# Decoder layer on one core: the near-Gram fold goes to GpSimd and ScalarE, the retrieval streams one block, two loads go behind the last row writes

## The chip, the cores and the metric

One Trainium2 chip, one core of it. The metric is the device time of one execution in microseconds (us); lower is better. Three runs of the kernel before gave a median of 910.58 us (910.43 to 911.65).

## The reference, cut to what matters

Input x is 8 x 512 x 256 in float32, with a context of the same shape and an integer mask of 8 x 512 x 512. Three blocks follow one another, each with a residual.

```
# block 1: layernorm twice, projection to q, k, v, beta (16 heads of 16), keys normalised
def step(S, (q_t, k_t, v_t, beta_t)):          # 512 steps, S: 16 x 16 per head and batch
    retrieval = S k_t
    S = S + outer(beta_t * (v_t - retrieval), k_t)
    return S, S q_t
x = x + (normed x + scan_out @ w_out + b_out)
# block 2: attention of layernorm(x) over the context, masked, then layernorm * gamma + beta
# block 3: int8-quantised activations (scale from a 99.5% quantile), ternary weights, gelu
```

## The kernel before, in words

**The scan.** The 512 steps are cut into 32 chunks (NCK) of 16 steps (CT). Inside a chunk the delta rule is a unit lower triangular system per head, batch and feature: the sixteen update vectors of the chunk depend on each other through the Gram matrix of the keys, scaled by beta. `solve(j)` on VectorE works it out by blocks: at t = 8 a block of 8 x 8 (the far Gram, straight from PSUM), at t = 4 and 12 blocks of 4 x 4, at t = 2, 6, 10 and 14 two steps at once against four earlier ones, at odd t single steps. Every step waits for the one before it.

For t = 2, 6, 10, 14 the coefficients lie in G3, which is prepared for the next chunk between two solves: `scale_near` multiplies the near Gram matrix in PSUM by beta (lines 1345 and 1347), `scale_pairs` writes the pair coefficients G4 (1353) and copies every second one, scaled, into G3 (1355), and `fold_near` adds the product of G3's first row and G4 to G3's second row (1363 and 1365). All that is VectorE's. In the same stretch VectorE normalises keys (1326), turns them (1395) and the updates (1331), and makes the key products for the next Gram matrices (`far_products` 1378, `near_products` 1388 and 1391, whose outputs TensorE sums by head). Its last act before the next solve is `start_chunk(m)` (1402), which waits for `ret_mm`.

**What start_chunk waits for.** TensorE does, in this order after a solve: `state` (the outer products into the state, 1902, waits for the turned updates), `turn` (2046), `values` (1998), `updates_turned` (1912) and `retrieval` (1941), whose last matmul raises `ret_mm`. The retrieval is 64 matmuls in float32 (two records each, 128 in the trace), four for each head, one on each diagonal 32 x 32 tile. The moving operand of a head is taken from `padded`, in which blocks of zeros lie between the blocks of keys and queries: it streams the zeros ahead of its own block, its own 32 columns and the zeros behind them (96 columns; 64 for the first and last head), so the neighbours' columns in PSUM get zeros added. Behind the retrieval, beside VectorE's solve, TensorE does `key_sums` (2007), attention within the chunk (1967) with the far Gram matmuls (1925) between its two parts, outputs (2024), projections (1976), the near Gram (1919, 1920), `norms_turned` (1951) and the output projection (2038).

**The other engines.** ScalarE, in chunk j: `updates_out` (710), `key_copied_out` (748), `state` (copies of the state by parity, 701, for which the retrieval waits), `updates_turned` (718), `queries_by_parity` (789), `scaled_by_feature` (780), `key_sums_out` (743), early work of later stages, then `attention_out` (726). GpSimd: `mask_attention` (537) as soon as the solve is done (`u_done`), the residual's bias (596), `x_added` (557), which releases the chunk's rows by `x_done`, and `key_norms` (547, 548, 550), which waits for ScalarE's line 743. These queues are in order; the order is written out by hand in each engine's block.

**SyncE's queue.** For each chunk it waits for `x_done` and writes eight blocks of rows to `xs` (471). At the last chunk it first waits for `u_done` and issues `context(2)`: the context and mask of the third batch, 0.5 and 1 MB (453, 454); after the last eight writes and `o_mm` it issues `context(3)`.

**After the scan.** 32 tiles of attention follow in a fixed order of steps (n). At step 2 VectorE runs `last_stats` (1419), which waits until all writes to the last quarter of `xs` have landed. `least(n)` (1443) is VectorE's part of the softmax, `logits` (2096) and `attend` (2117) TensorE's. The third batch's context is first read at steps 4 and 5 (`context_piece`, 2065).

Of the kernel before, what the change touches and what calls it, by code (L numbers as in the profile page):

```python
# [14 lines left out]
P = 128  # L15
# [120 lines left out]
def decoder(nc, x, ctx, mask, ln_g, ln_b, w_qkvb, b_qkvb, w_out, b_out, x_gamma, x_beta,  # L136
# [8 lines left out]
    with ExitStack() as stack:  # L145
# [75 lines left out]
        zeros = kexp_flat[:, 0:NH * 2 * HD]  # L221
        wq_s = wq_flat.rearrange("p (c n) -> p c n", c=DC)
# [161 lines left out]

        found, edge_marked, marks_summed = sem("found"), sem("edge_marked"), sem("marks_summed")
# [51 lines left out]
        def _(sp):  # L437
# [18 lines left out]
            for j in range(NCK):  # L456
                w, c = j // 8, j % 8
                if j == 21:
                    sp.wait_ge(tern_ready, 8)
                    for b in range(2):  # L460
                        context(b)
                if j == NCK - 2:
                    sp.wait_ge(ret_mm, NCK)
                    for t, vec in ((xg_s, x_gamma), (xb_s, x_beta), (fg_s, f_g), (fb_s, f_b)):
                        sp.dma_start(t[:, :], everywhere(vec)).then_inc(const_in, 16)
                if j == NCK - 1:
                    sp.wait_ge(u_done, NCK)
                    context(2)
                sp.wait_ge(x_done, j + 1)
                for b in range(B):  # L470
                    sp.dma_start(xs[c * CT:(c + 1) * CT, w * B + b, :], xc[b * CT:(b + 1) * CT, j, :]).then_inc(xs_in[w], 16)
            sp.wait_ge(o_mm, NCK)
# [14 lines left out]
        def _(pool):  # L487
# [99 lines left out]

            own(G.memset(half, -0.5))
# [3 lines left out]
            for j in range(NCK):  # L592
                pool.wait_ge(u_done, j + 1)
                mask_attention(j)
                pool.wait_ge(xr_ready, j + 1)
                G.tensor_tensor(xc[:, j, :], xc[:, j, :], bb_s, ALU.add).then_inc(xb_ready, 1)
                if j >= 1:
                    x_added(j - 1)
                if j + 3 < NCK:
                    key_norms(j + 3)  # L600
                if j in FACTORS_AT:
                    late_inputs(FACTORS_AT[j])
                if j in ROW_NORMS_AT:
                    row_norms(ROW_NORMS_AT[j])
                if 12 <= j < 16:
                    for p in range(2 * (j - 12), 2 * (j - 12) + 2):
                        bounded_weights(p)
# [84 lines left out]
        def _(act):  # L692
# [29 lines left out]
            def attention_out(j, f):  # L722
# [3 lines left out]
                A.activation(attn[j % 2][:, f * 512:(f + 1) * 512], ps[(2, 0)[f]][:, :], ACT.Copy).then_inc(att_out, 1)  # L726

# [300 lines left out]
            for j in range(NCK + 1):  # L1028
# [5 lines left out]
                if j >= 1 and exists(j):  # L1034
                    state(j)
                if exists(j - 1):
                    updates_turned(j - 1)
# [135 lines left out]
        def _(v):  # L1173
# [100 lines left out]
            def solve(j, between):  # L1274
# [6 lines left out]
                for t in range(1, CT):  # L1281
# [7 lines left out]
                    elif t % 4 == 2:  # L1289
                        a = t // 4  # L1290
                        part = prod[:, 0:NH * 8].rearrange("p (h t s) -> p h t s", t=2, s=4)
# [58 lines left out]
            def scale_pairs(m):  # L1350

                bt = beta[m % 4]
                own.issue(V.tensor_tensor(G4, psG[:, 768:896], bt.rearrange("p (q t) -> p q t", t=2)[:, :, 1], ALU.mult))
# [167 lines left out]
            for j in range(NCK + 1):  # L1521
# [24 lines left out]
                if exists(j + 1):  # L1546
                    fold_near(j + 1)
# [324 lines left out]
        def _(pe):  # L1872
# [55 lines left out]
            def retrieval(m):  # L1928
# [6 lines left out]
                for h in range(NH):  # L1935
                    if h % (NH // 2) == 0:
                        pe.wait_ge(state_copied, 2 * m - 1 + h // (NH // 2))
                    a, b = 1 if h == 0 else 0, 2 if h == NH - 1 else 3
                    for r in range(4):
                        rows = slice(32 * r, 32 * r + 32)  # L1940
                        last = M.matmul(into[rows, h - 1 + a:h - 1 + b], scopy[rows, h, :], streams[rows, h, a:b],  # L1941
# [216 lines left out]
            for j in range(NCK + 1):  # L2158
# [17 lines left out]
                if j == NCK:  # L2176
# [4 lines left out]
                    pe.wait_ge(ctxT_ready, 4)  # L2181
                if exists(j):
                    attention(j, 0)
                    far_gram(j, 0)
                    far_gram(j, 1)
                    attention(j, 1)
# [178 lines left out]
```

## Time and profile before

| What | us |
|---|---|
| median of 3 runs | 910.58 |
| profiled execution, whole | 912.2 |
| its span in the trace | 910.1 |
| busy in the span: TensorE, VectorE, ScalarE, GpSimd | 786.4, 763.6, 567.7, 439.8 |
| mean granted clock of TensorE, share of full | 0.952 |

The profile is of one execution, which took 912.2 us; 2.1 us of that lie outside the span. The scan runs from about 28 to 558 us of the span, the attention from there to about 720, the quantised block after it. The groups of instructions give a mean duration for each line; a line is that of the kernel's source. An engine's timeline shows in brackets how long it sat idle before a piece and what ended that. In the chain of waits each piece is what the end of the program really hung on at that moment.

### The profile page before, as it was taken

The numbers are of one execution on the slowest core, as the hardware profiler recorded it, in microseconds if no ns is written. First come the engines' busy times: TensorE is split into PE (matmuls) and PEld (weight loads), VectorE is DVE, ScalarE is ACT, GpSimd is POOL, SyncE is SP. The second block draws the span as 40 slices with busy tenths as digits, with TensorE's granted clock in tenths as the row PEclk, the third lists the DMA queues.
The fourth block names the chain that finished last, engine by engine and source line by source line (L and its number), as shares of the span: only waits on it lengthen the run. The fifth ranks groups of instructions, "written<-read, shape, count | busy, mean of one in ns | idle before, by whom it ended". The sixth has DMA issues, their size and how long they took to land.

```text
span 910.1 us, 31226 instructions
## 1 busy us (share of the span) xinstructions
PE 786.4 (86%) x12291; PEld 583.0 (64%) x12291; DVE 763.6 (84%) x2383; ACT 567.7 (62%) x1505; POOL 439.8 (48%) x472
## 2 busy tenths in 40 slices
PE   7799999999999999999999998799999506994385
PEld 7477777777777777777777776466666304442364
DVE  3789999999988999899899986566777786999897
ACT  4576777765766666667566644357777533993294
POOL 5346546643454545434435433548788733950000
PEclk9899999999999999999999999999999956997599
DMA  9800000000000000022000001432200000000023
GB/s 185 158 2 15 9 11 13 8 14 10 10 14 8 12 12 8 13 86 73 14 9 12 12 8 37 145 133 76 71 1 1 1 0 1 1 1 1 0 80 106
DMA packets 28616, 31.24 MB, mean 34 GB/s; under 512 B 5548, under 2 KB 23864, under 8 KB 28472
## 3 DMA queue, kind: packets, MB, share of 16 engines
q1 hardware_dynamic: 28256, 29.12, 12.1%
q8 instruction: 98, 1.61, 0.8%
q14 instruction: 46, 0.38, 0.1%
q10 hardware_dynamic: 216, 0.14, 0.1%
HBM read 20.85 MB, written 4.19 MB: 28 GB/s over the span
## 4 chain that ended last, share of the span: by engine, by line
DVE 48%; PE 42%; issue 6%; ACT 2%; POOL 1%; DVEq 0%; ACTq 0%; POOLq 0%
DVE arena L1306 7%; DVE arena L1314 7%; PE psY L1941 5%; PE ps L2096 4%; PE psX L1941 4%; DVE arena L1292 4%; DVE arena L1295 4%; PE ps L1902 3%; PE psX L2117 3%; DVE arena L1288 3%; DVE arena L1287 3%; DVE arena L1317 3%; PE psY L2117 2%; PE ps L2302 2%; PE psG L2096 2%
## 5 line engine op out<-in xcount | busy, mean ns | idle before, releaser
L537 POOL TENSOR_TENSOR arena<-arena 128x1024 f32<-128x1024 f32 x32 | 75.8, 2370 | 178.3 <-DVE arena L1295 178.3
L548 POOL TENSOR_TENSOR work<-work,half 128x16 f32<-128x16 f32 x32 | 97.9, 3061 | 2.7
L1314 DVE TENSOR_REDUCE arena<-arena 128x64 f32<-128x256 f32 (+1 forms) x96 | 65.9, 687 | 3.3
L1925 PE MATMUL psG<-arena 128*128 128x512 f32 x128 | 64.7, 629 | 0.0
L726 ACT ACTIVATE arena<-ps 128x512 f32<-128x512 f32 x64 | 34.7, 594 | 46.6 <-PE ps L1967 46.4
L547 POOL TENSOR_SCALAR work<-work 128x16 f32<-128x16 f32 x32 | 8.1, 252 | 103.7 <-ACT work L743 103.7
L1976 PE MATMUL ps<-arena 128*128 128x128 f32 x384 | 49.8, 279 | 2.9 <-ACT arena L726 1.5
L1976 PE MATMUL ps<-nT,arena 128*128 128x128 f32 x384 | 49.4, 279 | 3.3 <-ACT nT L780 1.2
L1976 PEld LDWEIGHTS ps<-arena 128*128 128x128 f32 x384 | 45.7, 192 | 6.3 <-ACT arena L726 5.5
L2096 PE MATMUL ps<-arena,nT 128*128 128x512 f32 x84 | 42.7, 632 | 7.6 <-issue 5.2
L1976 PEld LDWEIGHTS ps<-nT,arena 128*128 128x128 f32 x384 | 45.2, 192 | 5.9 <-ACT arena L726 4.4
L772 ACT ACTIVATE arena<-ps,columns 128x128 f32<-128x128 f32 x64 | 20.1, 364 | 45.6 <-PE ps L1976 45.6
L1902 PEld LDWEIGHTS ps<-work 32*32 32x32 f32 x1984 | 29.9, 105 | 26.6 <-issue 26.6
L1902 PE MATMUL ps<-work 32*32 32x64 f32 x1984 | 34.0, 215 | 14.7 <-DVE work L1331 14.7
L1967 PEld LDWEIGHTS ps<-work 32*64 32x64 f32 x1024 | 27.9, 132 | 28.3 <-issue 27.5
L1131 ACT ACTIVATE arena<-ps,small 128x512 f32<-128x512 f32 x64 | 41.8, 690 | 6.5 <-PE ps L2302 5.7
L1967 PE MATMUL ps<-work 32*64 32x128 f32 x1024 | 43.5, 282 | 2.1 <-ACT arena L780 1.8
L1941 PE MATMUL psY<-work,arena 32*32 32x96 f32 (+1 forms) x2048 | 44.4, 238 | 1.0 <-issue 0.6
L962 ACT ACTIVATE arena<-arena 128x512 f32<-128x512 f32 x32 | 23.1, 721 | 33.7 <-DVE arena L1443 33.6
L1941 PEld LDWEIGHTS psY<-work,arena 32*32 32x32 f32 x2048 | 41.5, 105 | 4.1 <-issue 4.1
L1306 DVE TENSOR_TENSOR arena<-psG,arena 128x1024 f32<-128x1024 f32 x32 | 39.2, 1224 | 4.3 <-PE psG L1925 3.2
L1941 PE MATMUL psX<-work,arena 32*32 32x96 f32 (+1 forms) x1920 | 41.6, 239 | 0.0
(358 smaller groups left out, 2410.2 us busy)
## 6 DMA issues: line engine op xcount, KB each, us to landing
arena<-in_mask_BxSxS_ik SPq DMA_DIRECT2D x8, 1024.0 KB, 6.7
xs<-arena SPq DMA_DIRECT2D x256, 16.0 KB, 1.9
arena<-in_ctx SPq DMA_DIRECT2D x8, 512.0 KB, 4.2
out<-xs SPq DMA_DIRECT2D x32, 128.0 KB, 1.7
arena<-in_x SPq DMA_DIRECT2D x8, 288.0 KB, 13.4
arena<-in_L_ffn_w SPq DMA_DIRECT2D x2, 1024.0 KB, 19.0
arena<-in_x SPq DMA_DIRECT2D x16, 96.0 KB, 5.2
arena<-in_L_attn_w_qkvb SPq DMA_DIRECT2D x2, 512.0 KB, 5.3
```

Source lines behind the costliest of these rows:

```text
L537: G.tensor_tensor(keys, keys, same_half.rearrange("p (a t) -> p a t", a=1).broadcast_to([P, NH, HALF]), ALU.mult).then_inc(att_masked, 1)
L548: own(G.tensor_tensor(root, length, half, ALU.pow))
L1131: A.activation(gT[:, n * 512:(n + 1) * 512], ps[n % 3][:, :], ACT.Gelu, scale=deq[:, 0:1]).then_inc(gabs, 1)
L1306: mult = V.tensor_tensor(part, src, C16[:, :, t - n:t].rearrange("p h (a s) -> p h a s", a=1).broadcast_to([P, NH, n, n]), ALU.mult)
L1314: own(V.tensor_reduce(sums, part, AX.X, ALU.add))
L1902: last = M.matmul(psS[rows, b * 64:b * 64 + 64], kt[rows, b * 32:b * 32 + 32], utm[rows, b * 64:b * 64 + 64], start=False, stop=True, skip ...
L1925: M.matmul(psG[:, f * 512:(f + 1) * 512], block16[:, :], PF[m % 2][:, f * 512:(f + 1) * 512], start=True, stop=True).then_inc(g1_mm, 1)
L1941: last = M.matmul(into[rows, h - 1 + a:h - 1 + b], scopy[rows, h, :], streams[rows, h, a:b], start=False, stop=True, skip_group_check=True)
L1967: last = M.matmul(ps[(2, 0)[r % 2]][tokens, first:first + P].rearrange("p (e t) -> p e t", e=2), kq[j % 4][rows, f * P + HALF * u:f * P + ...
L1976: last = M.matmul(out[:, f * P:(f + 1) * P], wq_s[:, c, first:first + P], nT[m % 4][:, c, :], start=c == 0, stop=c == DC - 1)
L2096: last = M.matmul(logit_bank(n), nT[n % 2][:, c, :], ctxT[b % 2][:, c, :], start=c == 0, stop=c == DC - 1)
L2117: last = M.matmul(psO[n % 2], probT[n % 2][:, u * P:(u + 1) * P], ctx_s[b % 4][:, u, :], start=u == 0, stop=u == NW - 1)
```

## The change

- `fold_near` for chunks from 1 on is taken from VectorE's block and put into GpSimd's, behind `mask_attention`; it writes a new scratch tile and GpSimd waits for `pre2` ahead of it and for its own first half ahead of the second. Chunk 0 keeps the old way.
- `scale_pairs` for chunks from 1 on issues one operation, G4; the copy of its odd entries into G3 becomes an activation on ScalarE, `pairs_copied_over`, behind the state copies.
- `solve(j)` waits at t = 2 for both.
- The retrieval streams one block, 32 columns, per matmul instead of up to three.
- In chunk 0 the two far Gram matmuls go ahead of the first half of the attention; in the other chunks the order is as it was.
- SyncE issues `context(2)` behind the last eight row writes, then `context(3)` with no wait on `o_mm`.

```diff
+        folded = kexp_flat[:, NH * 2 * HD:NH * 2 * HD + P]
...
-                if j == NCK - 1:
-                    sp.wait_ge(u_done, NCK)
-                    context(2)
                 sp.wait_ge(x_done, j + 1)
                 for b in range(B):
                     sp.dma_start(xs[...], xc[...]).then_inc(xs_in[w], 16)
-            sp.wait_ge(o_mm, NCK)
+            context(2)
             context(3)
...
+            def fold_near(m):                                    # GpSimd
+                pool.wait_ge(pre2, m + 1)
+                pairs = folded.rearrange("p (q s) -> p q s", s=2)
+                G.tensor_tensor(pairs, g3[:, :, 0, 0:2],
+                                G4.rearrange("p (q a b) -> p q a b", a=2, b=1)[:, :, 1].broadcast_to([P, NH * 4, 2]),
+                                ALU.mult).then_inc(folds, 1)
+                pool.wait_ge(folds, m)
+                G.tensor_tensor(g3[:, :, 1, 0:2], g3[:, :, 1, 0:2], pairs, ALU.add).then_inc(near_folded, 1)
...
                 mask_attention(j)
+                if j + 1 < NCK:
+                    fold_near(j + 1)
                 pool.wait_ge(xr_ready, j + 1)
...
+            def pairs_copied_over(m):                            # ScalarE
+                act.wait_ge(pre2, m + 1)
+                A.activation(G3.rearrange("p (q t s) -> p q t s", t=2, s=4)[:, :, 1, 2],
+                             G4.rearrange("p (q a) -> p q a", a=2)[:, :, 1], ACT.Copy).then_inc(pairs_copied, 1)
...
                     state(j)
+                    pairs_copied_over(j)
...
                     elif t % 4 == 2:                             # VectorE, solve
                         a = t // 4
+                        if t == 2 and j >= 1:
+                            v.wait_ge(near_folded, j)
+                            v.wait_ge(pairs_copied, j)
...
             def scale_pairs(m):                                  # VectorE
+                if m >= 1:
+                    V.tensor_tensor(G4, psG[:, 768:896], bt..., ALU.mult).then_inc(pre2, 1)
+                    return
...
-                if exists(j + 1):
-                    fold_near(j + 1)
...
-                    a, b = 1 if h == 0 else 0, 2 if h == NH - 1 else 3      # TensorE, retrieval
                     for r in range(4):
-                        last = M.matmul(into[rows, h - 1 + a:h - 1 + b], scopy[rows, h, :], streams[rows, h, a:b],
+                        last = M.matmul(into[rows, h], scopy[rows, h, :], streams[rows, h, 1],
...
+                if j == 0:
+                    far_gram(j, 0)
+                    far_gram(j, 1)
                 if exists(j):
                     attention(j, 0)
+                if exists(j) and j >= 1:
                     far_gram(j, 0)
                     far_gram(j, 1)
```

## Rows read from the trace of the kernel before

**Rows 1.** The page: busy us, share and instructions of each engine.
```profile
PE 786.4 (86%) x12291; PEld 583.0 (64%) x12291; DVE 763.6 (84%) x2383; ACT 567.7 (62%) x1505; POOL 439.8 (48%) x472
```

**Rows 2.** Chain of waits, end of one chunk's gap: start us, us, what.
```profile
331.38 2.71 PE psX L1941 x128
...
334.11 0.62 DVE arena L1402 x2
```

**Rows 3.** VectorE's timeline before the same start_chunk: start, us, engine, line, idle before.
```profile
330.49 0.25 DVE L1353 TENSOR_TENSOR arena<-psG,arena 128x128 f32<-128x128 f32 x1
330.67 0.26 DVE L1355 TENSOR_TENSOR arena<-psG,arena 128x64 f32<-128x64 f32 x1
330.84 1.21 DVE L1378 TENSOR_TENSOR arena<-ps,work 128x1024 f32<-128x1024 f32 x1
...
333.10 0.28 DVE L1363 TENSOR_TENSOR arena<-arena 128x128 f32<-128x128 f32 x1
333.41 0.29 DVE L1365 TENSOR_TENSOR arena<-arena 128x128 f32<-128x128 f32 x1
334.11 0.61 DVE L1402 SCALAR_TENSOR_TENSOR arena<-psX,columns,arena 128x128 f32<-128x128 f32 x2 [0.41 <-PE psX L1941]
```

**Rows 4.** Line 1402, whole span: idle before it by releaser, us and times.
```profile
  PE psY L1941: 9.3, 15
  PE psX L1941: 6.0, 14
```

**Rows 5.** VectorE, line 1402 of the last chunk.
```profile
547.21 0.61 DVE L1402 SCALAR_TENSOR_TENSOR arena<-psY,columns,arena 128x128 f32<-128x128 f32 x2 [2.44 <-PE psY L1941]
```

**Rows 6.** TensorE's timeline where that chunk's state update begins.
```profile
328.80 1.10 PE L1902 MATMUL ps<-work 32*32 32x64 f32 x64 [0.48 <-DVE work L1331]
```

**Rows 7.** TensorE by line and form, 200 to 400 us.
```profile
L1941 PE MATMUL psX<-work,arena 32*32 32x96 f32 x720 | 16.3, 241 | 0.0
L1902 PE MATMUL ps<-work 32*32 32x64 f32 x768 | 13.1, 215 | 5.8 <-DVE work L1331 5.8
```

**Rows 8.** GpSimd's and ScalarE's timelines, same chunk.
```profile
328.26 2.36 POOL L537 TENSOR_TENSOR arena<-arena 128x1024 f32<-128x1024 f32 x1 [5.93 <-DVE arena L1295]
...
334.89 0.25 POOL L547 TENSOR_SCALAR work<-work 128x16 f32<-128x16 f32 x1 [2.90 <-ACT work L743]
...
329.96 1.14 ACT L701 ACTIVATE arena<-ps,nparity 128x128 f32<-128x128 f32 x4 [0.24 <-PE ps L1902]
...
334.62 0.18 ACT L743 ACTIVATE work<-ps 128x16 f32<-128x16 f32 x1 [1.27 <-PE ps L2007]
```

**Rows 9.** Two windows: us, PE, PEld, DVE, ACT, POOL busy, clock, DMA share, GB/s.
```profile
240.00:360.00 120.00, 114.72 (x2430) 88.75 (x2419) 108.75 (x305) 78.57 (x237) 58.98 (x53) 1.00 0.05 11
...
584.00:586.00 2.00, 2.00 (x3) 0.97 (x4) 0.91 (x3) 0.82 (x2) 1.83 (x5) 0.50 0.02 4
```

**Rows 10.** Chunk 0: timelines of TensorE and VectorE.
```profile
33.05 0.67 PE L1967 MATMUL ps<-work 32*64 32x128 f32 x16 [1.85 <-ACT arena L780]
33.65 3.25 PE L1925 MATMUL psG<-arena 128*128 128x512 f32 x4
...
37.00 1.23 DVE L1306 TENSOR_TENSOR arena<-psG,arena 128x1024 f32<-128x1024 f32 x1 [3.25 <-PE psG L1925]
```

**Rows 11.** After the scan: SyncE's queue, then VectorE and TensorE.
```profile
568.70 0.51 SPq L454 DMA_DIRECT2D arena<-in_mask_BxSxS_ik  x1
569.25 4.96 SPq L471 DMA_DIRECT2D xs<-arena  x8
...
578.64 2.71 DVE L1419 BATCH_NORM_STATS2 stats<-xs 128x6 f32<-128x256 f32 x8 [4.06 <-DMA xs<-arena]
...
583.83 3.62 PE L2096 MATMUL ps<-arena,nT 128*128 128x512 f32 x4 [5.23 <-issue]
...
589.91 1.96 PE L2096 MATMUL ps<-arena,nT 128*128 128x512 f32 x4
```

**Rows 12.** The page: median time from issue to landing of the row writes.
```profile
xs<-arena SPq DMA_DIRECT2D x256, 16.0 KB, 1.9
```

More of the change, by code:

```diff
@@ L383, in decoder @@
              "h_ready h_last habs_ready cand_taken").split()]
+        folds, near_folded, pairs_copied = sem("folds"), sem("near_folded"), sem("pairs_copied")
         found, edge_marked, marks_summed = sem("found"), sem("edge_marked"), sem("marks_summed")
@@ L1352, in scale_pairs @@
                 bt = beta[m % 4]
+                if m >= 1:
+                    V.tensor_tensor(G4, psG[:, 768:896], bt.rearrange("p (q t) -> p q t", t=2)[:, :, 1],
+                                    ALU.mult).then_inc(pre2, 1)
+                    return
                 own.issue(V.tensor_tensor(G4, psG[:, 768:896], bt.rearrange("p (q t) -> p q t", t=2)[:, :, 1], ALU.mult))
@@ L2181, in _ @@
                     pe.wait_ge(ctxT_ready, 4)
+                if j == 0:
+                    far_gram(j, 0)
+                    far_gram(j, 1)
                 if exists(j):
                     attention(j, 0)
+                if exists(j) and j >= 1:
                     far_gram(j, 0)
                     far_gram(j, 1)
+                if exists(j):
                     attention(j, 1)
```

## The prediction

> **What bounds the kernel now.** I read the page first: TensorE and VectorE are both busy for over four fifths of the span [rows 1], so neither share says which one binds. The chain of waits does. In every chunk of the scan it runs through VectorE's solve, then TensorE's state update, values and retrieval, and back to `start_chunk` at line 1402. One chunk's gap between two solves ends with the retrieval, 2.71 us, and then line 1402 at 334.11 [rows 2]. VectorE's own timeline shows what it did meanwhile: its last preparation (1365) ended at 333.70, and it sat idle 0.41 us until TensorE's retrieval let it go [rows 3]. So two branches start at the end of a solve and meet at line 1402: TensorE's is the longer by 0.41 us, VectorE's is right behind. Over the whole span the idle time before line 1402 is 9.3 + 6.0 = 15.3 us in 29 waits [rows 4], 2.44 us of it in the last chunk [rows 5]. Chunk starts lie 16.41 us apart almost throughout. The reading that matters: a cut on VectorE alone gives nothing, a cut in the retrieval alone gives 0.4 us a chunk, both together give the smaller of the two new branches.
>
> **VectorE's branch.** Line 1355 goes: its successor starts 330.84 - 330.67 = 0.17 us behind it [rows 3]. Lines 1363 and 1365 go: from 333.10 to 333.70, 0.60 us. Together 0.77 us; with the idle 0.41 us, line 1402 can come 1.18 us earlier, if TensorE allows it. The two new waits at t = 2 cost nothing if they are met; the solve has such a wait at t = 8 already and its operation follows as closely as the others.
>
> **TensorE's branch.** 64 matmuls, 128 records, stream 32 columns in place of 96 (64 at the ends). No row has 32 columns on these tiles, so I work from two. `state` (1902) streams 64 columns in the same kind of tile, 64 records in 1.10 us [rows 6], each lasting 215 ns [rows 7]: (1100 - 215) / 63 = 14.0 ns from start to start, or 56 ns for each of the four tiles in turn. The retrieval: (2710 - 241) / 127 = 19.4 ns, 78 ns a tile. So 32 columns more cost 22 ns a tile, and 32 fewer should give 34 ns a tile, 8.6 ns a record: 127 x 8.6 + 200 = 1.29 us, a saving of 1.42 us. The bounds: nothing is saved if a record costs what it does now (2.71 us); if no record can follow another in less than the 14.0 ns of `state`, the retrieval takes 127 x 14.0 + 200 = 1.98 us and saves 0.73. I take 1.42, because both known forms lie on the line that streaming gives and neither shows a floor. The Trainium skill (TensorE: Matmul & The Clock Gate, "What overlaps and what doesn't" and the mechanism above it) puts the offset between matmuls on different tiles at about 4 ns, which would allow this; no row here has it.
>
> The smaller branch decides: VectorE's 1.18 us against TensorE's 1.42. VectorE becomes the bound, with TensorE 0.24 us behind. TensorE waits 0.48 us for the solve's result already [rows 6], so its work beside the solve has room.
>
> **GpSimd's and ScalarE's new work** I cost at nothing, and name the cover. GpSimd ends `mask_attention` at 330.62 [rows 8]; G4 is known at 330.49 + 0.25 = 330.74 [rows 3]. Two operations of 128 elements: between 0.25 us (16 elements, line 547) and 2.36 us (1024, line 537) each; by size 0.48 us [rows 8]. So the fold ends near 331.8; t = 2 of the next solve came at about 334.8 and will come at 333.6. Room: 1.8 us; with both operations at 1.3 us it is still met. Behind the fold wait the bias, `x_added` and through it SyncE's writes, which slip by 1.1 us, and `key_norms`, which sat idle 2.90 us for ScalarE anyway. ScalarE's copy of 64 elements lies between the 0.18 us of line 743 and the 0.29 us (1.14 / 4) of line 701 [rows 8]; I take 0.2. It stands behind the state copies (331.10), after G4 is known, so it adds no wait; what queues behind it is line 718, 789 and 780, and ScalarE then sat idle 1.27 us before line 743. That idle shrinks by 1.4 (earlier retrieval) and 0.2, to about nothing: this is what is late next, on a path (key norms) that has 3 us to spare on GpSimd.
>
> **The scan's sum.** Thirty periods end with `start_chunk(2)` to `(31)`. For 29 of them: 29 x 0.77 = 22.3 us, plus the idle that goes, 15.3 - 2.4 = 12.9, less about 1 us of the few waits well over 0.41 that TensorE's hiccups make and will make again: 34.2. The last chunk has no key work on VectorE, TensorE's branch binds there [rows 5], and it gains the 1.4 us of the retrieval. Scan: 35.6 us. TensorE's granted clock was 1.00 in the scan, the 2.4 GHz level, with TensorE busy 114.7 of 120 us [rows 9]; I take it as kept.
>
> **Chunk 0.** VectorE waited 3.25 us at t = 8 for the far Gram matmuls, which ran from 33.65 behind an attention part that had itself waited 1.85 us for ScalarE [rows 10]. Moved ahead they can run in that wait: the block starts at about 33.8 and not 37.0. The near Gram matmuls hang on VectorE's products behind that block, and the next keys on those, so all moves by 3.2 us; the 0.77 us comes on top, since VectorE bound that start too; and the far Gram (3.25 us here, against some 2 in later chunks) shows the 1.2 GHz level, part of which a shorter idle may give back: 0 to 1.3, I take 0.6. Chunk 0: 4.6 us (bounds 3.2 to 5.4).
>
> **After the scan.** SyncE issued `context(2)` just ahead of the last eight writes, and `last_stats` waited 4.06 us for those to land, at 578.64 [rows 11]. With the order turned round the writes are issued 1.2 us earlier and nothing large lies ahead of them: last issue near 573.0, landing 1.9 us later [rows 12], 574.9, against 574.6 when VectorE asks. Gain 3.7 us. TensorE idled 5.23 us there, and the next four matmuls took 3.62 us in place of 1.96 [rows 11], with a granted clock of 0.50, the 1.2 GHz level [rows 9]. With 1.5 us of idle that should not fall: 1.6 us. The moved loads: context and mask of two batches issue behind the writes, about 5 us later than `context(2)` did; they are read from step 4, near 590, and land by 584 or so. Cover gone, it would cost the difference. Sum 5.3 us (bounds 0 to 5.7).
>
> **Total.** 35.6 + 4.6 + 5.3 = 45.5. The profiled execution took 912.2, so 866.7; that execution is 1.6 above the median, so against the median 865.1. I say 866.
>
> **Rivals.**
> - *A floor under the small matmuls.* If a record costs 14.0 ns however few its columns, TensorE's branch saves only 0.73 us: 29 x 0.73 + 0.7 + 4.6 + 5.3 = 32, which gives 879; floors between put it between. For it: no denser row exists. Against: `state` sits just where its 64 columns put it, so 14.0 need not be a floor. The Trainium skill (TensorE: Matmul & The Clock Gate, "Wait — 56ns, not 53.3ns?") says start-to-start never drops below about 25 ns however small N is. If that held across tiles, 128 records would take 3.2 us, more than now; the 14.0 ns of `state` speak against it.
> - *The retrieval gains nothing* (nothing saved per record, or the edit is not what limits it). Then only chunk 0 and the end gain: 912.2 - 9.9 = 902.
> - *The clock falls: slower.* The streamed zeros keep TensorE occupied. If less activity let the clock go to 1.2 GHz through state, values and retrieval, 1.10 + 1.48 + 1.29 = 3.87 us would double: per chunk 3.87 - 1.42 = 2.45 us worse than now, 30 x 2.45 - 10 = +64, so 976. It decides once the clock costs over 1.5 us a chunk. Against: TensorE stays busy nearly throughout, and the clock was seen low only after idle of several us [rows 9, 11].
> - *The new wait at t = 2 replaces the old one.* If GpSimd's pair took 3.8 us in place of 1.0, it would cost about 1 us a chunk: 895.
>
> **How the numbers follow.** Forecast case (VectorE binds, 860 to 870): 0.52. Floor (870 to 884): 0.30. No gain from the retrieval or a late fold (885 to 905): 0.10. Slower by the clock: 0.05. No measurable change: 0.02. The rest is better than 860. The range 860 to 884 holds the first two. A measurement of this kernel tells 0.2%, 1.8 us, from nothing: faster 0.93, same 0.02, slower 0.05.
>
> **What would show it.** Chunk starts 15.2 us apart; the idle before line 1402 gone but in the last chunk; the retrieval near 1.3 us with 8 to 9 ns a record; no idle at line 1292 for GpSimd; the far Gram of chunk 0 ahead of 33; `last_stats` idle under 0.5 us and the matmuls behind it at 1.96. I am wrong if the idle before line 1402 stays (floor), if line 1292 shows a wait, or if the granted clock in the scan leaves 1.00.

## The result, and the profile after

The changed kernel takes 902.9 us (median of 4: 901.5, 902.4 and 903.3 at a mean granted clock of 0.927, and 927.9 at 0.900) against 910.5: a ratio of 0.9909 [0.9884, 0.9933], 8.3 us less. The forecast was 866.0, with a range of 860 to 884. Medians here and below take in every execution of a kernel; ratios and their intervals leave out those that lie over 1.5% above the fastest one of their kernel. The profiled execution took 901.47 us, with a span of 899.6. The page:

```profile
PE 766.0 (85%) x12284; PEld 548.1 (61%) x12291; DVE 743.7 (83%) x2290; ACT 572.5 (64%) x1536; POOL 465.2 (52%) x534
PE 47%; DVE 40%; issue 7%; ACT 4%; POOL 1%; DVEq 0%; ACTq 0%; POOLq 0%
PEclk9889998998999999999999999999999757997599
```

VectorE has 20 us less to do and GpSimd 25 more, as the fold would have it [rows 1]. TensorE's busy time is the odd one: the retrieval is busy 43.9 us where it was 85.9, 42 less, and TensorE as a whole only 20 less. In the line of the granted clock the scan, slices 2 to 24, has four slices under 0.9; before it had one. Two windows of the scan say where (us, then PE, PEld, DVE, ACT, POOL busy, granted clock, DMA share, GB/s):

```profile
120.00:240.00 120.00, 112.26 (x2397) 79.05 (x2396) 100.85 (x274) 78.37 (x254) 63.51 (x69) 0.90 0.05 10
240.00:360.00 120.00, 112.68 (x2581) 84.33 (x2582) 110.86 (x301) 85.88 (x263) 70.59 (x70) 1.00 0.05 12
```

The second answers to [rows 9]: clock 1.00, as before. In the first it is 0.90, and VectorE is busy a tenth less in the same time. So there are chunks of two kinds. One where the clock holds, TensorE's and VectorE's timelines:

```profile
253.93 0.59 DVE L1427 SCALAR_TENSOR_TENSOR arena<-psY,columns,arena 128x128 f32<-128x128 f32 x2
257.94 1.22 DVE L1327 TENSOR_TENSOR arena<-psG,arena 128x1024 f32<-128x1024 f32 x1
...
254.07 0.61 PE L2029 MATMUL ps<-arena 128*128 128x8 f32 x4 [0.21 <-DVE arena L1416]
254.61 0.67 PE L1989 MATMUL ps<-work 32*64 32x128 f32 x16
255.20 1.98 PE L1948 MATMUL psG<-arena 128*128 128x512 f32 x4
```

Line 1427 is `start_chunk` (1402 before). It follows with no idle time in front of it, and so does the operation at t = 8 (1327), which needs the far Gram matmuls (1948, before 1925). And one where it falls, first TensorE, then VectorE (the operation at t = 8, and `keys_normed` behind the solve), then TensorE's clock microsecond by microsecond:

```profile
166.93 1.29 PE L1963 MATMUL psX<-work,arena 32*32 32x32 f32 x128
169.10 0.61 PE L2029 MATMUL ps<-arena 128*128 128x8 f32 x4 [0.89 <-DVE arena L1416]
169.64 0.68 PE L1989 MATMUL ps<-work 32*64 32x128 f32 x16
170.25 3.63 PE L1948 MATMUL psG<-arena 128*128 128x512 f32 x4
...
173.99 1.23 DVE L1327 TENSOR_TENSOR arena<-psG,arena 128x1024 f32<-128x1024 f32 x1 [1.05 <-PE psG L1948]
181.93 0.42 DVE L1347 TENSOR_TENSOR work<-work,ps 128x256 f32<-128x256 f32 x1 [0.66 <-ACT arena L752]
```

```profile
169.00:170.00 1.00, 0.90 (x16) 0.88 (x20) 0.93 (x5) 0.25 (x2) 0.23 (x1) 1.00 0.00 0
170.00:171.00 1.00, 1.00 (x13) 0.43 (x9) 0.90 (x3) 0.97 (x3) 0.90 (x2) 0.72 0.07 16
171.00:172.00 1.00, 1.00 (x3) 0.36 (x2) 0.90 (x4) 0.97 (x4) 1.00 (x1) 0.50 0.19 47
172.00:173.00 1.00, 1.00 (x3) 0.30 (x1) 0.84 (x4) 0.77 (x3) 1.00 (x1) 0.50 0.09 18
```

The retrieval takes the forecast 1.29 us. Behind it TensorE is idle for 0.89 us, waiting for VectorE's key products (1416), runs key sums and attention at full speed, and then the granted clock drops to 0.50, the 1.2 GHz level. The four far Gram matmuls take 3.63 us in place of 1.98. VectorE waits 1.05 us for them at t = 8, and 0.66 us more at `keys_normed`, since TensorE's work behind them, and with it ScalarE's keys (752), is late too. That is 1.71 of the 1.8 us by which such a chunk is longer: chunk starts lie 15.22 us apart where the clock holds and nothing else comes in, and 17.0 where it falls. Only six of the nineteen periods without a slow group are that short (15.21 to 15.26); the middle one of the nineteen is 15.53.

Of the 31 far Gram groups behind a retrieval 11 are slow, 16.7 us in all; before the change none is. There is a second loss. In the scan from 60 us on, 12 gaps on TensorE of over 0.45 us (11.7 us in all) wait for no other engine; before there is one, of 0.64 us. One of them, in TensorE's timeline:

```profile
217.96 1.19 PE L1963 MATMUL psY<-work,arena 32*32 32x32 f32 x117
220.78 0.31 PE L1963 MATMUL psY<-work,arena 32*32 32x32 f32 x11 [1.64 <-issue]
```

What these gaps wait for can be read from the traces all the same. The page counts the packets that carry instructions, here for the changed kernel and for `half_32` below, whose TensorE has 3472 records less:

```profile
q8 instruction: 98, 1.61, 0.8%
```

```profile
q8 instruction: 85, 1.39, 0.7%
```

That is 16 KB a packet, one for every 250 or so of TensorE's 24575 matmul and weight-load records, and 13 packets less for 3472 records less: queue 8 carries TensorE's instructions. Count all that the trace has of TensorE, its waits included, in the order of the starts. All 79 gaps of over 0.45 us in the scans of fourteen profiles, those of the two kernels and of every run below, end at the same place in a block of 256: at number 193, 194 or 195, counted from 0. Each of them also ends 1.2 to 1.6 us behind the end of a packet on that queue, a stretch that takes up 7% of the changed kernel's scan. The one above ends 1.42 us behind a packet that took 0.94 us. So TensorE stands at the edge of a block and waits for the next one. From 60 us on the scan has 81 such edges, and 30 of them lie inside a retrieval, which with its weight loads is 256 records long and now takes 1.29 us instead of 2.74.

After the scan, SyncE's queue, `last_stats` on VectorE (1444, before 1419 in [rows 11]) and the logits behind it:

```profile
554.72 10.44 SPq L470 DMA_DIRECT2D xs<-arena  x16
565.21 0.58 SPq L455 DMA_DIRECT2D arena<-in_ctx  x1
567.40 2.71 DVE L1444 BATCH_NORM_STATS2 stats<-xs 128x6 f32<-128x256 f32 x8
572.59 1.96 PE L2118 MATMUL ps<-arena,nT 128*128 128x512 f32 x4 [1.21 <-issue]
```

The writes are issued ahead of the context, `last_stats` no longer waits, and the matmuls behind it take 1.96 us, not 3.62, behind an idle time of 1.21 us, not 5.23.

**Where the time went**, from one profile to the other, by chunk starts: the lead-in 0.1 us less; chunk 0, 25.22 to 22.78, 2.4 less; the thirty periods behind it, 493.79 to 489.17, 4.6 less; from the end of the last solve to the second set of logits behind `last_stats` 5.7 less. That is 12.9 us, of which 10.5 is left at the end of the span: behind those logits the first 110 us are the same in both (TensorE busy 106.81 us), and in the 80 us behind them, in the quantised block, the granted clock is 0.70 in place of 0.74. Most of the miss is in the thirty periods: 4.6 us in place of 35.6, which is 31.0 of the 34.8 us by which the profiled execution missed the forecast.

### The profile page after: what moved, and what is told of

Read it like the earlier page. It is cut to its first block, busy times and chain, and to the rows that moved or that the text cites. A ratio compares the mean times of both kernels' runs of the same rounds, so it can differ in the third digit from the quotient of the medians.

```text
span 899.6 us, 31219 instructions
## 1 busy us (share of the span) xinstructions
PE 766.0 (85%) x12284; PEld 548.1 (61%) x12291; DVE 743.7 (83%) x2290; ACT 572.5 (64%) x1536; POOL 465.2 (52%) x534
## 4 chain that ended last, share of the span: by engine, by line
PE 47%; DVE 40%; issue 7%; ACT 4%; POOL 1%; DVEq 0%; ACTq 0%; POOLq 0%
PE ps L1998 5%; PE psG L1948 5%; PE ps L2118 4%; DVE arena L1327 4%; DVE arena L1335 4%; PE psX L2139 3%; PE psY L2139 3%; PE ps L2329 2%; PE ps L1989 2%; DVE arena L1403 2%; DVE arena L1313 2%; DVE arena L1316 2%; PE psG L2118 2%; DVE arena L1413 2%; PE psG L1942 2%
## 5 line engine op out<-in xcount | busy, mean ns | idle before, releaser
L547 POOL TENSOR_TENSOR work<-work,half 128x16 f32<-128x16 f32 x32 | 95.9, 2998 | 2.7
L1948 PE MATMUL psG<-arena 128*128 128x512 f32 x128 | 80.0, 758 | 0.0
L1327 DVE TENSOR_TENSOR arena<-psG,arena 128x1024 f32<-128x1024 f32 x32 | 39.2, 1224 | 15.2 <-PE psG L1948 14.4
L1989 PE MATMUL ps<-work 32*64 32x128 f32 x1024 | 46.0, 292 | 4.1 <-issue 3.9
L1948 PEld LDWEIGHTS psG<-arena 128*128 128x128 f32 x128 | 25.6, 220 | 26.6 <-issue 26.6
L1313 DVE TENSOR_TENSOR arena<-arena 128x128 f32<-128x128 f32 x128 | 37.9, 296 | 4.4
L1316 DVE TENSOR_REDUCE arena<-arena 128x32 f32<-128x128 f32 x128 | 36.6, 286 | 4.4
L2329 PE MATMUL ps<-work 128*128 128x512 bf16 x124 | 37.9, 385 | 2.2 <-ACT work L1144 2.1
```

The lines of the kernel that those rows point to most:

```text
L547: own(G.tensor_tensor(root, length, half, ALU.pow))
L1313: own(V.tensor_tensor(part, g3h[:, :, a].rearrange("p h (t s) -> p h t s", s=4), C16[:, :, 4 * a:4 * a + 4].rearrange("p h (a s) -> p h a ...
L1316: last = V.tensor_reduce(C16[:, :, t:t + 2], part, AX.X, ALU.add)
L1327: mult = V.tensor_tensor(part, src, C16[:, :, t - n:t].rearrange("p h (a s) -> p h a s", a=1).broadcast_to([P, NH, n, n]), ALU.mult)
L1948: M.matmul(psG[:, f * 512:(f + 1) * 512], block16[:, :], PF[m % 2][:, f * 512:(f + 1) * 512], start=True, stop=True).then_inc(g1_mm, 1)
L1989: last = M.matmul(ps[(2, 0)[r % 2]][tokens, first:first + P].rearrange("p (e t) -> p e t", e=2), kq[j % 4][rows, f * P + HALF * u:f * P + ...
```

## The experiments

Each run is compared with runs of the kernel before on the same chip (medians 910.7, 911.2 and 910.7 us in the three batches). The table is read from the profiled executions: typical distance of two chunk starts; slow far Gram groups (over 2.4 us) of the 31 behind a retrieval; gaps of TensorE inside a retrieval of over 0.45 us that wait for no other engine. Each count is of one execution. Two runs, the halved retrievals, are single executions.

| kernel | us, median | ratio | start to start, us | slow groups (extra us) | gaps |
|---|---|---|---|---|---|
| before | 910.5 | | 16.41 | 0 | 1 |
| changed | 902.9 | 0.9909 [0.9884, 0.9933] | 15.22 / 17.0 | 11 (16.7) | 8 |
| before_32 | 924.4 | 1.0055 [1.0011, 1.0098] | 15.9 / 17.2 | 15 (23.2) | 6 |
| after_96 | 902.6 | 0.9912 [0.9888, 0.9936] | 16.41 | 1 (1.2) | 1 |
| after_64 | 888.1 | 0.9765 [0.9707, 0.9822] | 15.66 | 1 (1.2) | 5 |
| after_48 | 888.6 | 0.9734 [0.9677, 0.9792] | 15.3 to 15.9 in most | 4 (5.2) | 4 |
| after_fill2 | 896.3 | 0.9816 [0.9755, 0.9876] | 15.5 to 18 | 6 (8.6) | 12 |
| after_fill4 | 907.8 | 0.9948 [0.9909, 0.9988] | 16.0 | 1 (1.8) | 11 |
| half_96 | 869.2 | (one execution) | 15.35 | 1 (1.2) | 0 |
| half_32 | 919.3 | (one execution) | 17.05 | 27 (40.1) | 3 |
| sp_only | 907.4 | 0.9958 [0.9931, 0.9984] | 16.40 | 0 | 0 |
| far_only | 906.7 | 0.9957 [0.9932, 0.9983] | 16.41 | 0 | 0 |
| after_again | 911.4 | 0.9899 [0.9836, 0.9962] | 15.36 / 17.0 | 15 (23.0) | 6 |
| after_64_again | 891.0 | 0.9796 [0.9729, 0.9863] | 15.66 | 0 | 3 |

The two theories at the start: (A) the short retrieval leaves TensorE too little to do and its clock falls; (B) the fold, or the waits it added, is what makes some chunks long.

### One half of the change at a time: before_32 and after_96

`before_32` is the kernel before with the short retrieval alone, `after_96` the changed kernel with the old, wide one. The edit of the first; the second is its reverse:

```diff
-                    a, b = 1 if h == 0 else 0, 2 if h == NH - 1 else 3
                     for r in range(4):
                         rows = slice(32 * r, 32 * r + 32)
-                        last = M.matmul(into[rows, h - 1 + a:h - 1 + b], scopy[rows, h, :], streams[rows, h, a:b],
+                        last = M.matmul(into[rows, h], scopy[rows, h, :], streams[rows, h, 1],
                                         start=False, stop=True, skip_group_check=True)
```

> The kernel before with one edit: the retrieval streams only its own 32 columns. Theory (too little work passes through TensorE around the retrieval, so the granted clock falls behind it): the clock in the scan leaves 1.00 in part of the chunks, the far Gram matmuls of those take 3.6 us in place of 1.98, and the gain of 0.4 us a chunk that VectorE leaves (12 us in all) is eaten or more: 905 to 925 us. Rival (the clock falls only with the fold gone from VectorE, or with the new waits on GpSimd and ScalarE): the clock stays at 1.00, chunk starts 16.0 us apart, about 898 us.

> The changed kernel with the old retrieval of up to 96 columns, everything else kept. Theory (columns of the retrieval hold the clock): granted clock 1.00 through the scan, chunk starts 16.4 us apart, VectorE idle some 1.2 us before start_chunk, and about 902 us from chunk 0 and the end alone: no slower than the changed kernel. Rival (the moved fold, its waits or the shortened VectorE work disturb the clock): clock under 1.00 in the scan here too and over 910 us.

The short retrieval by itself makes the old kernel slower, by 0.6% [0.1, 1.0] in the ratio and by 1.5% in the median. Its ten executions take 910.8 to 949.6 us, with a mean granted clock of 0.885 to 0.933; the 24 of the kernel before beside it all have 0.947 to 0.954. Its slow and fast chunks are like those of the changed kernel, one of the slow ones on TensorE's timeline:

```profile
103.31 1.29 PE L1940 MATMUL psX<-work,arena 32*32 32x32 f32 x128
...
106.81 3.68 PE L1925 MATMUL psG<-arena 128*128 128x512 f32 x4
```

There is no fold on GpSimd in this kernel and no wait for it, so (B) falls. And the fold without the short retrieval leaves chunk starts at 16.41 us: VectorE's 0.77 us turn into idle time in front of `start_chunk`, as its waits show (us, times):

```profile
  PE psY L1964: 24.3, 16
  PE psX L1964: 15.9, 15
```

That is 40.2 us against 15.3 before [rows 4], or 24.9 more in 31 waits, 0.80 each (one gap of TensorE of 3.1 us is in it). All of this kernel's 8 us come from the two other parts of the change.

### A retrieval between the two: after_64, after_48

`after_64` streams 64 columns of every head, one block of zeros beside the head's own. `after_48` does that for odd heads and 32 for even ones.

```diff
+                    a, b = (1, 3) if h < NH - 1 else (0, 2)    # after_64
+                    a, b = (1, 2) if h % 2 == 0 else (0, 2)    # after_48
...
-                        last = M.matmul(into[rows, h], scopy[rows, h, :], streams[rows, h, 1],
+                        last = M.matmul(into[rows, h - 1 + a:h - 1 + b], scopy[rows, h, :], streams[rows, h, a:b],
```

> The changed kernel, but each matmul of the retrieval streams 64 columns, its own block and one block of zeros. By the line through 64 and 96 columns it takes 1.98 us, chunk starts 15.7 us apart, VectorE idle 0.4 us before start_chunk. Theory: with TensorE busy without a gap the clock holds, and 30 x 0.73 us come on top of what 96 columns give: about 880 us, below both kernels. Rival (the clock needs all 96 columns, or idle is not what matters): the clock falls in part of the chunks and it lands between 890 and 905 us.

> The changed kernel with 32 columns for even heads and 64 for odd ones: the retrieval takes some 1.6 us. Theory: chunk starts 15.3 us apart where the clock holds; whether it holds lies between the changed kernel (often not) and the form of 64 columns (nearly always): 875 to 890 us. Rival (any retrieval under 64 columns loses the clock as often as the changed kernel): 900 us and more.

Both beat both kernels, though `after_64` stays 8 us above the 880 expected: its thirty periods are 16.0 us long on average, not 15.7, mostly for gaps in five of its retrievals and three behind them. With 64 columns TensorE is the bound again, and the clock stays. From `after_64`, the timelines (retrieval and far Gram matmuls, then `start_chunk` between them), and a window of the scan with the columns as above:

```profile
251.45 1.99 PE L1964 MATMUL psX<-work,arena 32*32 32x64 f32 x128
254.50 1.98 PE L1948 MATMUL psG<-arena 128*128 128x512 f32 x4
...
253.50 0.61 DVE L1427 SCALAR_TENSOR_TENSOR arena<-psX,columns,arena 128x128 f32<-128x128 f32 x2 [0.36 <-PE psX L1964]
```

```profile
240.00:360.00 120.00, 114.63 (x2510) 86.74 (x2508) 108.70 (x296) 83.52 (x257) 68.18 (x70) 1.00 0.05 12
```

128 records in 1.99 us, (1990 - 215) / 127 = 14.0 ns each: the price of `state`. Chunk starts lie 15.66 us apart, 0.75 less than before, where the floor rival had said 0.73. The columns that are now streamed for nothing cost 0.44 us a chunk against the 15.22 of a chunk that keeps its clock, and spare the 1.8 us of one that doesn't. The one slow group comes behind a gap; the four of `after_48` are more than that and fewer than 11, in one execution each.

### More work behind the short retrieval: after_fill2, after_fill4

The changed kernel with two or four matmuls of 128 columns and zero weights behind each retrieval; they add nothing to the result.

```diff
                     retrieval(j)
+                    for _ in range(2):    # 4 in after_fill4
+                        M.matmul(psR[(j - 1) % 2][:, 0:P], zeros[:, 0:P], ones[:, :], start=False, stop=True,
+                                 skip_group_check=True)
```

> The changed kernel (32 columns) with 2 extra matmuls of 128 columns (zero weights, added to a bank nobody reads then) right behind the retrieval, where TensorE sat idle 0.5 to 0.9 us: 4 records, about 0.45 us. Theory (the clock falls because TensorE does too little between the state update and the far Gram): the falls get fewer, chunk starts 15.2 us apart where it holds; 870 to 890 us. Rival (what counts is the retrieval itself): as the changed kernel, 903 us.

> The same with 4 extra matmuls, about 0.9 us, as long as TensorE's idle time. Theory: the clock stays at 1.00 throughout, chunk starts 15.2 us apart, 30 x 1.18 us on top of chunk 0 and the end: about 866 us, what I had forecast for the change. Rival: as the changed kernel, 903 us, or worse by what the extra work delays (0.2 us a chunk, 6 us).

The number of slow groups goes from 11 to 6 and to 1 with the work added, which again speaks for (A). The times don't follow: 896.3 us lies above the 870 to 890 expected, and 907.8 us is what the rival had said, not 866. The work stands in TensorE's queue ahead of key sums and attention, ScalarE's keys come late (with four, `keys_normed` waits 12.7 us in 22 chunks), the gaps stay, and what the clock gives back goes there. The ten executions of `after_fill4` are spread over 897 to 913 us, with a mean granted clock of 0.949 down to 0.928. The profiled one is the fastest, with the 0.949, so the single slow group says little of the others, and that four matmuls hold the clock is shown for that execution alone.

### Clock or gaps: half_96, half_32

Slow groups and gaps came together so far. These two part them. Both are the changed kernel with the retrieval of nine heads only (72 matmuls; that of the other seven is left out), one with 96 columns and one with 32:

```diff
+                    if h % 2 and h < NH - 1:
+                        continue
+                    a, b = 1 if h == 0 else 0, 2 if h == NH - 1 else 3    # half_96
+                    a, b = 1, 2                                           # half_32
```

> The changed kernel with a retrieval for nine of the sixteen heads only (the even ones and the last; the retrieval of the other seven is left out), each streaming up to 96 columns: 72 records instead of 128, about 1.5 us. Two things are told apart, by the trace of the scan alone: the gaps over 0.45 us inside or behind the retrieval in which TensorE waited for nothing shown (12 in the changed kernel, 1 in the one before), and the clock. Theory (the gaps come where instructions are used up faster than they arrive): with 72 in place of 128 records at 20 ns each the gaps all but vanish, 0 to 3. The clock then holds in nearly all chunks, starts 15.2 to 15.4 us apart. Rival (the gaps belong to the shorter cycle or to something else that the change added): some ten gaps again.

> The same nine heads with 32 columns each: 72 records in about 0.75 us; the other seven heads' retrieval is left out. Theory of the clock: it falls at least as often as in the changed kernel (11 of 31 chunks with far Gram matmuls over 2.4 us), now with few gaps, so that the fall needs no gap: 10 or more slow chunks. Rival (the clock falls only behind such a gap): as the gaps vanish, so do the slow chunks.

The same instructions on every engine, and 50 us between them: 869.2 and 919.3. TensorE's timeline of one chunk, first with 96 columns (the row names the 64 of its first head), then with 32:

```profile
308.75 1.58 PE L1966 MATMUL psX<-work,arena 32*32 32x64 f32 x72
310.61 0.61 PE L2032 MATMUL ps<-arena 128*128 128x8 f32 x4 [0.28 <-DVE arena L1416]
311.15 0.67 PE L1992 MATMUL ps<-work 32*64 32x128 f32 x16
311.75 1.99 PE L1948 MATMUL psG<-arena 128*128 128x512 f32 x4
```

```profile
304.98 0.82 PE L1966 MATMUL psX<-work,arena 32*32 32x32 f32 x72
307.15 0.61 PE L2032 MATMUL ps<-arena 128*128 128x8 f32 x4 [1.35 <-DVE arena L1416]
307.69 0.67 PE L1992 MATMUL ps<-work 32*64 32x128 f32 x16
308.29 3.68 PE L1948 MATMUL psG<-arena 128*128 128x512 f32 x4
```

and VectorE at t = 8 of the second, 312.08:

```profile
312.08 1.22 DVE L1327 TENSOR_TENSOR arena<-psG,arena 128x1024 f32<-128x1024 f32 x1 [1.09 <-PE psG L1948]
```

In both VectorE sets the pace: in front of `start_chunk` it waits for TensorE once, in the last chunk. The retrieval's shorter time only makes TensorE idle for longer, 1.35 us in place of 0.28, and right behind that the clock falls, in 27 of 31 chunks. Over 240 to 360 us (columns as above, `half_96` first):

```profile
240.00:360.00 120.00, 115.41 (x2214) 86.82 (x2214) 112.52 (x309) 86.83 (x269) 70.41 (x72) 1.00 0.05 11
```

```profile
240.00:360.00 120.00, 110.20 (x2001) 77.31 (x2001) 99.10 (x268) 76.82 (x235) 60.34 (x65) 0.88 0.04 10
```

So the clock alone, with hardly a gap (three in 31 retrievals), takes a chunk from 15.35 to 17.05 us. The thirty periods last 511.6 us in place of 463.3, 48.3 of the 50.1 us. The loss stays 1.7 us even where less of the slow stretch falls on the far Gram group: in chunk 28 that takes 3.13 us, VectorE waits only 0.54 us for it, and then 1.11 us at `keys_normed`. The other way round, `half_96` has no gap and one slow group, in chunk 1, and lands at 869.2 us where the sum of the prediction had come to 866: with the clock kept, the rest of that sum holds. What the pair can't tell apart is the streaming that is gone and the idle time that takes its place; the one always turns into the other here. In 31 retrievals of 72 records there are no such gaps with 96 columns and three with 32; in 31 of 128 records with 32 columns six and eight. The block edges fit: with 72 records 15 of them lie inside a retrieval, with 128 it is 30. A gap comes where a long row of tiny matmuls uses up its instructions faster than the next block arrives. No run changed how they arrive.

### The two parts outside the scan: sp_only, far_only

`sp_only` is the kernel before with the context and mask of the third and fourth batch moved behind the last writes, `far_only` the kernel before with chunk 0's far Gram matmuls ahead of its attention.

```diff
-                if j == NCK - 1:
-                    sp.wait_ge(u_done, NCK)
-                    context(2)
...
-            sp.wait_ge(o_mm, NCK)
+            context(2)
             context(3)
```

```diff
+                if j == 0:
+                    far_gram(j, 0)
+                    far_gram(j, 1)
                 if exists(j):
                     attention(j, 0)
+                if exists(j) and j >= 1:
                     far_gram(j, 0)
                     far_gram(j, 1)
```

> The kernel before with one edit: the third batch's context and mask are issued behind the last eight row writes. Theory: last_stats no longer waits 4.06 us, the matmuls behind it run at 1.96 us and not 3.62: 5.7 us less, 904.9 us. Rival (the DMA queues were the bound, or the loads now come too late): under 2 us of change.

> The kernel before with one edit: in chunk 0 the far Gram matmuls go ahead of the first half of the attention. Theory: VectorE's wait of 3.25 us at t = 8 of chunk 0 goes, but part comes back ahead of keys_normed, since the projections behind it run at half clock: 1.5 to 3 us less. Rival (all of it comes back): no change.

They are worth 0.42% [0.16, 0.69] and 0.43% [0.17, 0.68], 3.8 and 3.9 us, and their sum is the 8 us of `after_96`. In `sp_only` the wait of `last_stats` is gone and the logits behind it follow sooner (VectorE, then TensorE):

```profile
573.52 2.71 DVE L1416 BATCH_NORM_STATS2 stats<-xs 128x6 f32<-128x256 f32 x8
...
578.71 1.96 PE L2093 MATMUL ps<-arena,nT 128*128 128x512 f32 x4 [1.21 <-issue]
583.13 1.96 PE L2093 MATMUL ps<-arena,nT 128*128 128x512 f32 x4
```

From the set of logits ahead of it (568.75) to the second behind it (583.13) is 14.38 us, where it was 589.91 - 569.84 = 20.07: the 5.7 us are there, and the changed kernel has 14.38 as well. The profiled span is 5.7 us shorter too, but over ten executions only 3.8 are left, and I can't say where the rest goes. `far_only` gains more than the 1.5 to 3 us expected: it takes chunk 0 from 25.22 to 20.53 us, with VectorE's t = 8 no longer idle and the projections behind it at full clock:

```profile
29.84 1.88 PE L1925 MATMUL psG<-arena 128*128 128x512 f32 x4
...
32.59 1.22 DVE L1306 TENSOR_TENSOR arena<-psG,arena 128x1024 f32<-128x1024 f32 x1
...
37.09 1.10 PE L1919 MATMUL psG<-arena 128*128 128x512 f32 x2 [1.77 <-issue]
```

The changed kernel has the same order there, and its profile the same gap of 1.78 us, but a clock of 0.50 behind it, so that the same two matmuls take 2.05 us, and the wait that comes after is long (TensorE, then VectorE):

```profile
38.15 2.05 PE L1942 MATMUL psG<-arena 128*128 128x512 f32 x2 [1.78 <-issue]
41.26 1.92 PE L1998 MATMUL ps<-arena 128*128 128x128 f32 x8
...
46.77 0.42 DVE L1347 TENSOR_TENSOR work<-work,ps 128x256 f32<-128x256 f32 x1 [4.70 <-ACT arena L752]
```

`after_64`, with the same order again, has 19.85 us there, 5.4 less than before. One execution each can't say how often chunk 0 meets the low clock.

### Once more: after_again, after_64_again

The changed kernel and `after_64` unedited.

> The changed kernel as it is, a second time. Theory: the median stays within 3 us of 902.9, and the number of slow far Gram chunks lies near 11 of 31 again, though not in the same chunks. Rival (the fall of the clock was a single profile's): another number altogether.

> The form with 64 columns again, on the same chip as the changed kernel beside it: 888 us, 14 us below it, with at most 3 slow far Gram chunks. Rival (its gain was the chip's): under 5 us between the two.

The expectation for the changed kernel failed in its median: 911.4 us and not 902.9. Its four executions take 898.6 and 905.0 us at a mean granted clock of 0.927 and 0.925, and 917.9 and 918.3 us at 0.908. The profiled one, at 917.9, has 15 slow groups, 23.0 us in all. So the gain of 1% in the ratio is that of the executions in which the clock falls less often; with all of them the kernel is no faster here than the one before, at 910.7. The rival, that the falls were a single profile's, is out. `after_64` stands: 891.0 us, 20 us below the changed kernel, a ratio of 0.9796 where it was 0.9765, chunk starts 15.66 us apart again and no slow group at all. Its eight executions, on two chips, take 886.0 to 897.4 us.

## Why the prediction was wrong, step by step

**What bounds the kernel** was right: two branches meet at `start_chunk`, TensorE's longer by 0.41 us. `after_96` shows that a cut on VectorE's branch alone gives nothing, as the text had it. That a cut in the retrieval alone gives 0.4 us a chunk (0.5 measured) holds only where the clock does: 16.41 to 15.9 in such chunks of `before_32`.

**The retrieval** was right where nothing interrupts it: 1.29 us, 8.6 ns a record, in 11 of 31 chunks. The last digit is luck: the 19.4 ns belong to 92 columns on average, since two of the sixteen heads stream 64, and the same working with 92 gives 7.8 ns and 1.19 us. Streaming goes on being the price at 32 columns; 64 columns cost 14.0 ns. The floor of about 25 ns from start to start that the Trainium skill states (TensorE: Matmul & The Clock Gate, "Wait — 56ns, not 53.3ns?") doesn't show for matmuls on four tiles in turn: 8.6 ns. On one tile the distance is 34 ns, so no run here tests the floor for a single tile.

**VectorE's branch**, 1.18 us a chunk: 16.41 - 15.22 = 1.19 where the clock holds and no gap comes in. The fold was costed rightly too:

```profile
251.83 0.45 POOL L591 TENSOR_TENSOR arena<-arena 128x128 f32<-128x128 f32 x1 [0.33 <-DVE arena L1375]
252.37 0.46 POOL L595 TENSOR_TENSOR arena<-arena 128x128 f32<-128x128 f32 x1
251.86 0.34 ACT L742 ACTIVATE arena<-arena 128x64 f32<-128x64 f32 x1
```

0.45 and 0.46 us against 0.48, and no wait at t = 2. The room was larger than I had it: before the change t = 2 of that solve came at 335.20, not at 334.8. ScalarE's copy takes 0.34 us where I took 0.2, over my upper row, and it cost nothing.

**The clock is the step that failed.** "TensorE's granted clock was 1.00 in the scan, the 2.4 GHz level, with TensorE busy 114.7 of 120 us [rows 9]; I take it as kept." It wasn't: `half_96` against `half_32` shows the fall with nothing else changed. The mistake in the argument is that I took busy time for the condition, and took the low clock to come only after idle of several us. TensorE is still busy 112.3 of 120 us, with less than 1 us idle in front of the fall shown above; what went was 64 of 96 columns in 128 of its matmuls, and some idle time in place of them. I had put this among the rivals, and there three things were off. The place: the clock falls behind the retrieval, at the far Gram matmuls, not through state, values and retrieval. The price: about 1.8 us for a chunk that it hits, measured from a period of 15.22, so such a chunk is 0.6 us *longer* than before and a spared one up to 1.2 shorter; 11 of 31 are hit, 15 in `after_again`. My 2.45 us for every chunk gave 976. The chance: 0.05, when no row spoke of the clock with so few columns. Worth noting is that "it decides once the clock costs over 1.5 us a chunk" is about where it does decide: at 27 hit chunks (`half_32`) the kernel is slower than before, at 15 (`after_again`, 917.9 us) too, at 11 it gains a little.

The miss in the scan, 35.6 - 4.6 = 31 us, is then about 20 us for 11 slow groups at 1.8 us a chunk, and about 11 us for the gaps inside and around the retrieval. VectorE's idle time closes the sum: in the thirty periods it waits 14.4 us at t = 8, 9.4 us at `keys_normed` and 7.9 us in front of `start_chunk`, 31.7 us in all. The cut between clock and gaps is an estimate, as two gaps, of 1.97 and 1.37 us, lie in front of slow far Gram groups and so inside waits at t = 8. **The gaps** are a second term, and it was mis-sized: they were in the text only as the "hiccups" behind "about 1 us of the few waits", and came to ten times that, because the shorter retrieval reaches the edge of an instruction block before the next one is there.

**No gain from the retrieval** was forecast at 902 us, the time that came out. It is the right number by the wrong way: the retrieval's busy time fell by 42.0 us in 31 chunks, 1.35 each, and the clock and the gaps took the gain back.

**Chunk 0**, 4.6 us (3.2 to 5.4): 2.4 in the profile of the changed kernel, whose clock was low there, 4.7 in `far_only`, which has only the moved block, and 5.4 in `after_64`. The mechanism is right; a low clock behind a gap was costed on the wrong side, as a possible gain alone.

**After the scan**, 5.3 us: 5.7 measured in the profile, by the step named, the wait and the clock behind it; over the ten executions of `sp_only` it is 3.8. Of the moved loads nothing is seen.

## What to carry to other kernels

Work that an engine does for nothing, beside a bound on another engine, may be what keeps its clock. Where a change takes streaming out of TensorE, price the low clock at the *next* large matmuls, not only at those that were cut, and try sizes in between: here 64 columns of 96 keep the clock and about half of the gain forecast (ratio 0.9765), and 32 lose most of it (0.9909), and all of it in half of the executions of `after_again`. A row of tiny matmuls also uses up its instructions faster: see whether the gaps in it lie a whole number of 256 instructions apart. A total that fits one theory's number is no evidence for it, and a single profile may be the fastest of a kernel whose executions differ by 2%; look for the distance of two chunk starts and see whether there is one or two of them.

## What the runs showed that was not expected

- The clock falls although TensorE is busy 92% of a chunk and idle for no more than 1.4 us in most: `half_32` in 27 of 31 chunks, behind 0.82 us of retrieval and 1.35 us of idle; the changed kernel in 11. What picks a single chunk stays open: in the changed kernel it was kept at 236.07 behind a retrieval of 1.29 us and 1.36 us of idle time, and lost at 149.87 behind one with a gap of 0.58 us and 0.11 us of idle time. Slow chunks come in rows, seven of them from 115 to 218 us.
- Matmuls on four small tiles in turn follow each other in 8.6 ns with 32 columns and in 14.0 ns with 64, in the mean of a retrieval.
- A retrieval of 128 records with 32 columns lasts 1.6 us or more, and not 1.29, in 17 of 31 chunks, mostly for gaps at the edge of an instruction block. With 96 columns, before the change, two of 31 were over their 2.74 by 0.3 us or more.
- TensorE's long gaps with no other engine in front of them all end at the same place in a block of 256 of its records, 79 of 79, and 1.2 to 1.6 us behind the end of a 16 KB instruction packet.
